# A graph network's message pass: one picked slot in twelve instead of fifteen, and an end that fetches its rows plainly and early

## The reference, cut to what matters

```python
def _L1_gnn_ref(node_feats, edge_index, edge_sh, edge_radial, W1, b1, ...):
    src, dst = (edge_index[0], edge_index[1])
    msg_input = jnp.concatenate([node_feats[src], edge_sh, edge_radial], axis=-1)   # 64 + 9 + 8
    h = jax.nn.silu(msg_input @ W1 + b1)          # 128
    h = jax.nn.silu(h @ W2 + b2)                  # 128
    messages = h @ W3 + b3                        # 64
    aggregated = jax.ops.segment_sum(messages, dst, num_segments=node_feats.shape[0])
    update_input = jnp.concatenate([node_feats, aggregated], axis=-1)
    gate = jax.nn.sigmoid(update_input @ G + gb)
    u = jax.nn.silu(_layernorm(update_input @ U1 + ub1, ln1_g, ln1_b))
    update = _layernorm(u @ U2 + ub2, ln2_g, ln2_b)
    return node_feats + gate * update
```

## Time and profile before

| | |
|---|---|
| median of 3 runs | 3172.85 us (3168.97 to 3183.3) |
| the profiled execution, its own time | 3195.68 us |
| its span, first to last instruction | 3194.0 us |
| mean granted TensorE clock | 0.925 of full |
| busy | PE 86%, DVE 60%, ACT 51%, POOL 47% |
| counting stage | 130 to 655 us |
| message pass | 1207 to about 3061 us |
| fetches of the end | 3063.7 to 3155.5 us |

### The profile page before, as it was taken

How to read it: one execution, slowest core, us unless ns; L and a number is a source line. 1 busy time by engine, 2 the same in 40 slices (tenths; PEclk the granted TensorE clock), 3 DMA queues, 4 the chain that set the end, 5 groups by cost and what they waited for, 6 DMA issues and landing times.

```text
span 3194.0 us, 63519 instructions
## 1 busy us (share of the span) xinstructions
PE 2752.0 (86%) x20761; PEld 2179.8 (68%) x20761; DVE 1919.2 (60%) x2346; ACT 1613.8 (51%) x2994; POOL 1515.6 (47%) x1572
## 2 busy tenths in 40 slices
PE   4499999967999985889888989888989898898975
PEld 3377777757998982666666666666767666676654
DVE  5899999964444564455555555555555555555526
ACT  2488888832332223455545555545555554555534
POOL 4000000000000006777777777777777777777765
PEclk9999999968999996899999999999999999999976
DMA  3133333326998973445444445544445555444421
GB/s 109 61 141 161 141 161 141 161 121 260 365 361 320 359 287 79 107 121 132 120 119 119 122 117 125 129 121 121 121 117 125 119 128 124 120 121 116 126 48 30
DMA packets 216659, 477.09 MB, mean 149 GB/s; under 512 B 53932, under 2 KB 114910, under 8 KB 197601
## 3 DMA queue, kind: packets, MB, share of 16 engines
q1 hardware_dynamic: 159976, 422.33, 38.5%
q0 software_dynamic: 55632, 52.47, 10.3%
q10 hardware_dynamic: 1001, 1.66, 0.1%
HBM read 339.87 MB, written 136.41 MB: 149 GB/s over the span
## 4 chain that ended last, share of the span: by engine, by line
PE 47%; POOL 25%; issue 11%; DVE 11%; DMA 4%; ACT 1%; DVEq 0%; POOLq 0%; ACTq 0%
POOL arena L663 22%; PE ps L791 14%; PE ps L961 8%; PE ps L810 6%; PE ps L973 5%; PE ps L980 5%; PE ps L988 5%; DMA arena<-m_tab,m_idx 3%; DVE arena L1868 2%; POOL ybuf L678 2%; PE ps L950 2%; DVE stageT L1844 2%; PE ps L706 1%; PE ps L694 1%; POOL arena L604 0%
## 5 line engine op out<-in xcount | busy, mean ns | idle before, releaser
L663 POOL DMA_INDIRECT arena<-m_tab,m_idx x1463 | 1391.4, 951 | 1586.0 <-issue 1574.8
L2118 DVE TENSOR_TENSOR_SCAN arena<-arena,ps 128x512 f32<-128x512 f32 x391 | 500.2, 1279 | 856.6 <-ACT ps L1335 723.4
L988 PEld LDWEIGHTS ps<-weights,arena 128*128 128x128 f32 x3128 | 438.2, 203 | 210.3 <-issue 196.4
L1330 ACT ACTIVATE arena<-ps,weights 128x512 f32<-128x512 f32 x391 | 268.7, 687 | 490.7 <-PE ps L973 483.1
L791 PE MATMUL ps<-arena 128*128 128x195 bf16 (+1 forms) x4802 | 481.5, 248 | 32.2 <-DVE arena L1810 31.6
L791 PEld LDWEIGHTS ps<-arena 128*128 128x128 f16 x4802 | 416.8, 98 | 62.8 <-DVE arena L1810 31.8
L961 PE MATMUL ps<-ends,arena 128*128 128x192 bf16 x4900 | 458.9, 252 | 0.0
L973 PE MATMUL ps<-arena,weights 81*128 81x512 f32 x782 | 443.5, 651 | 0.0
L980 PE MATMUL ps<-arena,weights 128*128 128x512 f32 x782 | 435.9, 640 | 0.0
L961 PEld LDWEIGHTS ps<-ends,arena 128*128 128x128 bf16 x4900 | 421.7, 100 | 7.0
L988 PE MATMUL ps<-weights,arena 128*128 128x64 f32 x3128 | 415.4, 279 | 1.7 <-ACT arena L1342 1.7
(11 more groups left out here) (269 smaller groups left out, 2294.1 us busy)
## 6 DMA issues: line engine op xcount, KB each, us to landing
arena<-count_d SPq DMA_DIRECT2D x98, 1568.0 KB, 8.5
arena<-keep_d SPq DMA_DIRECT2D x391, 256.0 KB, 3.9
count_d<-arena SPq DMA_DIRECT2D x49, 1568.0 KB, 5.1
scan_rows<-arena SPq DMA_DIRECT2D x391, 128.0 KB
arena<-m_tab,m_idx POOLq DMA_INDIRECT x1463, 3.3
arena<-attr_in SPq DMA_DIRECT2D x391, 34.0 KB
arena<-src_row SPq DMA_DIRECT2D x25, 258.0 KB
hT_d<-stageT ACTq DMA_DIRECT2D x12, 132.0 KB
```

Of the source, the lines that this page charges most:

```text
L663: pool.indirect_dma_start(m_rows[:, k, t, :], None, m_tab, bass.IndirectOffsetOnAxis(ap=m_idx[:, k, t:t + 1].bitcast(U32), axis=0))\
L988: last = pe.matmul(m_back[k % BACK_RING][:, t * D:(t + 1) * D], m_scan[:, k % SCAN_RING, t * P:(t + 1) * P], W("W3"), start=True, stop=True)
L2118: dve.tensor_tensor_scan(m_scan[:, k % SCAN_RING, :], m_mask[:, k % MASK_RING, :], m_term[k % TERM_RING], before, ALU.mult, ALU.add).then_ ...
```

## The change

- `LOOP` goes from 15 to 12: 33 laps instead of 27, 31 of them in the inner loop instead of 25, each with one picked slot. The first lap has 12 gathered slots instead of 15, the last 7 instead of 1. Rings are resized to divide 12.
- The nine picks of a lap stand in PE's slots 5 to 9, two each in four of them; the 0/1 pieces are made in DVE's slots 0 to 3 (three, two, two, two).
- The last four `rows_back` write to three PSUM banks instead of one.
- SP writes zeros to the last 20 slots of `scan_rows` once the masks are stored: 10240 rows of 256 bytes, all read from one row on one SBUF partition.
- The fetches of the end don't add any more. Each group waits only until as many slots are stored as its last node needs (a number that DVE computes and POOL loads into a register), so that they follow the last gather at once. DVE adds the b3 term, now kept in `hbuf`, per group (`add_b3`). POOL's adds to the residual rows stay behind all fetches.

```diff
-LOOP = 15
+LOOP = 12
-MASK_RING = 5
-ATTR_RING, TERM_RING, SCAN_RING, OUT_RING = 5, 3, 5, 5
+MASK_RING = 6
+ATTR_RING, TERM_RING, SCAN_RING, OUT_RING = 4, 3, 4, 4
+CLEARED = 20
-IDX_STEP = 5
+IDX_STEP = 4
-PICK_RING, PICK_BLOCKS, PICK_LAG = 3, 6, 5
+PICKS_AT = {5: (0, 1), 6: (2, 3), 7: (4, 5), 8: (6, 7), 9: (8,)}
+MARKS_AT = {0: (0, 1, 2), 1: (3, 4), 2: (5, 6), 3: (7, 8)}
+JOIN_AT = 7
...
             sp.wait_ge(masks_stored, 6 * DMA)
+            sp.dma_start(scan_rows[(NSLOT - CLEARED) * BE:NSLOT * BE, :], zero_row[:, :].unsqueeze(1).to_broadcast([1, CLEARED * BE, D]))\
+              .then_inc(zero_stored, DMA)
...
-            for k in range(OUT_RING):
-                pool.wait_ge(e1.stored[k], DMA * ((NSLOT - k + OUT_RING - 1) // OUT_RING))
             for i, (a, n) in enumerate(END_GROUPS):
+                needed = slots_needed[P - 1:P, a + n - 1:a + n]
+                pool.wait_ge(e1.turn_done, LOOP * (LAPS - 1) + fetch_slots[i] + 1 + (LOOP if fetch_slots[i] < LAST else 0))
+                pool.wait_ge(e1.out_ready, pool.to_reg(pool.value_load(needed, min_val=OUT_RING + 1, max_val=NSLOT + OUT_RING)))
+                pool.sem_inc(alone, 1)
                 for j in range(a, a + n):
                     pool.indirect_dma_start(ybuf[:, j, :], None, scan_rows,
-                                            bass.IndirectOffsetOnAxis(ap=end_idx[:, j:j + 1].bitcast(U32), axis=0),
-                                            compute_op=ALU.add).then_inc(rows_fetched[i], DMA)
+                                            bass.IndirectOffsetOnAxis(ap=end_idx[:, j:j + 1].bitcast(U32), axis=0))\
+                        .then_inc(rows_fetched[i], DMA)
...
-                    if PICK_LAG <= k < PICK_LAG + len(PICKS):
-                        pick_rows(i, k - PICK_LAG)
+                    for n in PICKS_AT.get(k, ()):
+                        pick_rows(i, n)
...
+            def add_b3(i, a, n):
+
+                dve.wait_ge(rows_fetched[i], fetched[i] + n * DMA)
+                dve.tensor_tensor(ybuf[:, a:a + n, :], ybuf[:, a:a + n, :], hbuf[:, a:a + n, :], ALU.add).then_inc(agg_ready, 1)
```

More of the change, by code:

```diff
@@ L258, in build @@
         m_back = [ps[:, 2 + TERM_RING, k * TB * D:(k + 1) * TB * D] for k in range(BACK_RING)]
+        last_back = [ps[:, 2 + TERM_RING + k % 3, 0:TB * D] for k in range(LAG)]
         def W(name):
@@ L397, in late_block @@
             return first % RING, first // RING + k + 1, first + RING * k
-        update_ready, hT_stored, hT_loaded, let_in = (sem(n) for n in ("update_ready", "hT_stored", "hT_loaded", "let_in"))
+        update_ready, hT_stored, hT_loaded, agg_ready = (sem(n) for n in ("update_ready", "hT_stored", "hT_loaded", "agg_ready"))
         agg_turned, agg_copied, agg_multiplied = (sem(n) for n in ("agg_turned", "agg_copied", "agg_multiplied"))
-        rows_fetched = e1.gathered[1:1 + len(END_GROUPS)]
-        FETCHED = DMA * TB * (LAPS - 1)
+        fetch_slots = [*range(LAST, PICKED), *range(1, 1 + len(END_GROUPS) - (PICKED - LAST))]
+        rows_fetched = [e1.gathered[k] for k in fetch_slots]
+        fetched = [DMA * TB * (LAPS if k < LAST else LAPS - 1) for k in fetch_slots]
         u_ready, u_squared, u_staged, u_turned, u_done, gate_done, v_done, v_added, v_squared = (sem(n) for n in (
             "u_ready", "u_squared", "u_staged", "u_turned", "u_done", "gate_done", "v_done", "v_added", "v_squared"))
+        let_in = sem("let_in")
         zero_ready, zero_stored = sem("zero_ready"), sem("zero_stored")
@@ L563, in move_slot @@
                     load_mask(s - LAG + MASK_RING, (k - LAG) % MASK_RING)
+            sp.wait_ge(zero_stored, 2 * DMA)
             for k in range(LOOP):
@@ L575, in _ @@
                 store_rows_of(s, s % OUT_RING)
+            for k in range(OUT_RING):
+                sp.wait_ge(e1.stored[k], DMA * ((NSLOT - k + OUT_RING - 1) // OUT_RING))
+            sp.sem_inc(e1.out_ready, OUT_RING)
             for i, (a, n) in enumerate(END_GROUPS):
@@ L980, in hidden_out, with rows_back @@
                 pe.matmul(m_term[k % TERM_RING], W("W2"), m_hid[:, k % HID_RING, :], start=True, stop=True).then_inc(e1.w2_done, 1)
-            def rows_back(s, k, late):
+            def rows_back(s, k, late, to=m_back[0], ring=BACK_RING):
                 pe.wait_ge(e1.scan_done, s + 1)
                 if late:
-                    pe.wait_ge(e1.out_ready, s - BACK_RING + 1)
+                    pe.wait_ge(e1.out_ready, s - ring + 1)
                 for t in range(TB):
-                    last = pe.matmul(m_back[k % BACK_RING][:, t * D:(t + 1) * D], m_scan[:, k % SCAN_RING, t * P:(t + 1) * P], W("W3"),
+                    last = pe.matmul(to[:, t * D:(t + 1) * D], m_scan[:, k % SCAN_RING, t * P:(t + 1) * P], W("W3"),
                                      start=True, stop=True)
@@ L1018, in _ @@
                 hidden_out(s, s % LOOP, True)
-            for s in range(NSLOT - LAG, NSLOT):
-                rows_back(s, s % LOOP, True)
+            for n, s in enumerate(range(NSLOT - LAG, NSLOT)):
+                rows_back(s, s % LOOP, True, last_back[n], n + 1 if n < 3 else 3)
             flat = ones[:, :].bitcast(BF16)
@@ L1034, in turn_agg @@
                     keep_busy(3, 8)
-                pe.wait_ge(rows_fetched[i], FETCHED + n * DMA)
+                pe.wait_ge(agg_ready, i + 1)
                 for t in range(n):
@@ L1335, in second_silu, with rows_out @@
                 act.activation(m_term[k % TERM_RING], m_term[k % TERM_RING], ACT.Silu, bias=W("b2")).then_inc(e1.silu2_done, 1)
-            def rows_out(s, k, lap):
+            def rows_out(s, k, lap, of=m_back[0]):
                 act.wait_ge(e1.back_done, s + 1)
@@ L1368, in _ @@
                 second_silu(s, s % LOOP)
-            for s in range(NSLOT - LAG, NSLOT):
-                rows_out(s, s % LOOP, s // LOOP)
+            for n, s in enumerate(range(NSLOT - LAG, NSLOT)):
+                rows_out(s, s % LOOP, s // LOOP, last_back[n])
             def square_u(i, a, n):
@@ L2140, in _ @@
                     scan_slot(LOOP * i + k, k, i)
-                    if k < len(PICKS):
-                        mark_pick(i, k)
+                    for n in MARKS_AT.get(k, ()):
+                        mark_pick(i, n)
             for k in range(LAST):
```

19 lines of the change are left out of this document (14 added, 5 removed).

## The result

The changed kernel takes 3149.24 us (median of 20 runs, 3133.78 to 3170.45), the kernel before 3184.72 us on the same chips (20 runs, 3168.64 to 3195.43). The ratio is 0.9902, 95% interval 0.9882 to 0.9922: 1.0% faster. The time forecast was 3149 us, and that agreement is luck. The forecast said 24 us less, and measured were 35.5 us less; the three runs from which it started (median 3172.85) lay 12 us under the median of the 20, which hides just this. The profiled execution says the same as the medians: span 3158.3 us against 3194.0, 35.7 less.

A forecast was written before the change was run, and what follows sets the result against it. POOL's gathers were taken to bound the message pass, and the fetches the node update at the end. Loop -30, end -26 and zeros +32 gave -24 from 3172.85 to 3149 us; forecast's own range 3135 to 3168, overall 3110 to 3204.

The forecast's parts named there:

- The loop, -30: Message pass: 1439 gathers instead of 1463, 24 fewer at 1.25 us, -30.0 us if PE keeps up.
- 4.6 us of slack: Message pass: PE needs 50.4 us of POOL's 55.0 us lap, so slack falls from 10.8 to 4.6 us.
- the pieces just in time: Message pass: DVE makes each 0/1 piece in 1.80 us with 2 us available, so picks hold with little to spare.
- The risk that was given 0.04: Message pass, rival 3: PE becomes the loop's bound and gathers wait for its turnings, +81 us, 3230 us; chance 0.04.
- The end, -26: From last gather's end to span's end: 124 us instead of 150.0, with fetches no longer kept waiting; bounds -34 and -10.
- first bias add T + 27: End: DVE's first bias add comes 27 us after T, the end of the last gather, where it was T + 39.
- eight steps 72: End, node update: nine groups have eight steps between them, taken at 9.0 us each, 72 us.
- The write of zeros, +32: Before the counting stage's block stores: a 94 us write delays block 0 and stops ACT at block 2, +32 us.
- The bound of 298 us: Write of zeros: upper duration for one source partition, by doubling from a 64-partition load of 11.4 us.
- The formula: Write of zeros: start 87 + duration 94 + landing 5.1 - 154.1, when ACT begins block 2, gives +32 us.
- Rival 1: Write of zeros is hidden, lasting 62 us or less: -56, 3117 us; chance 0.25.
- Rival 4: End: the update keeps today's pace of 11.0 us a step, losing 16 us of the gain, 3165 us; chance 0.09.

The follow-up runs named there:

- the version with 128 partitions: Changed kernel with its zeros read from a zero row in each of 128 partitions instead of one: median 3107.2 us, ratio to before 0.9767.
- the four kernels with a stop: Changed kernel, and it with the zero row 128 B further on, with 2 KB pieces, or with ACT issuing the write: medians 3149.2, 3145.0, 3145.1, 3158.9 us.
- the two kernels with 27 GB/s in SP's queue: Changed kernel with the zero row 128 B further on, or with zeros in 2 KB pieces, both from one partition: ratios to before 0.9871 and 0.9880.

## Why the prediction was right, and where it was not

**The loop, -30: right.** Measured -32.1 us; four more traces have 1802.2 to 1804.5 us. The premise of 4.6 us of slack in a lap on PE held (4.1 waited), and so did the pieces just in time. The risk that was given 0.04, gathers that wait for PE's turnings, is real on a chip that holds PE back, and was not thought of as a matter of the chip.

**The end, -26: right in kind, too small; -47.0.** The terms, forecast against measured: first bias add T + 27 against T + 20.7; eight steps 72 against 60.1; the add rows 2 more, not seen apart; last bias add to the end 23.2 against 22.1. Two terms were mis-sized. The first is the way to the first bias add: the last turning back ended at T + 12.5 instead of T + 14.4, and with PE at work the granted clock stood at 1.00 between 3060 and 3110, where in before it was 0.67 from 3054 to 3064, so that the filler went in 4.5 us instead of 6.0 and the first turning reached its bias add in 4.0 us instead of 6.7. The prediction let the clock pass for a thing that "may" rise.

The larger one, 12 us, is the duration of a group's step: 9.0 us forecast, 7.5 on the mean. It was read from two steps of before as if their data had been ready. Four windows, each from one bias add to the next: the 8.9 us step of before, the fifth and the seventh step of after, and the seventh with 128 partitions:

```profile
3106.03:3114.94 8.91, 4.72 (x36) 4.22 (x34) 4.99 (x9) 5.87 (x9) 7.39 (x6) 1.00 0.21 18
```

```profile
3103.78:3111.74 7.96, 5.35 (x39) 4.82 (x37) 7.51 (x16) 6.24 (x9) 6.13 (x7) 0.98 0.15 28
3119.95:3128.30 8.35, 3.71 (x25) 3.12 (x26) 8.11 (x15) 6.03 (x9) 2.88 (x3) 1.00 0.21 76
```

```profile
3061.46:3069.81 8.35, 6.33 (x25) 5.59 (x26) 8.11 (x16) 6.03 (x9) 2.88 (x3) 0.59 0.21 76
```

In the step of before DVE was busy 5.0 of 8.9 us and PE 4.7, and the steps beside it took 12.8 and 14.1: these three went at the pace of the fetches, 11.0 us a group, or slower, and were no measure of the update's own work. (The other step that was read, 8.3 us, is the last one, of a small group; it took 7.9 in after.) In after DVE is busy 7.3 to 8.1 us in each step from the fourth to the seventh, which take 7.6 to 8.4, so DVE's work sets them. The clock does not: the seventh step takes 8.35 us at 1.00 and at 0.59 alike. The first two take 6.5 us, with DVE busy 4.0 and 4.5; the normalising of earlier groups comes in only later. The register loads that the prediction put at 0.8 us a group leave no idle time that shows (0.30 us between fetches, 49 times); 49 fetches end 63 us behind T instead of 68. What ends last now is DVE, with the fetches close behind: DVE waited 0.2 us for one at 3111.2.

**The write of zeros, +32: right in kind, too small; +43.5.** The term that was mis-sized is its duration: 94 us, scaled from a table store of 512 such rows, against 113.6. That 94 lies so near is in part luck: nothing in the table store has to do with a single source partition, which is what sets the time. (The bound of 298 us is no bound either: it doubles the 64-partition time four times, and from 64 partitions to one are six doublings.) The formula with the measured figures gives 85.3 + 113.6 + 5.1 - 154.1 = 49.9, and the last block store is 50.6 us later. Of that 7.1 us came back before the first gather. This was not foreseen: the 90 us behind the last block store had the clock at 0.56 before and 0.72 after. The gain comes only with a stop (from the last block store to first gather 553.2 us in before and 554.6 with 128 partitions, 545.2 to 546.3 in the four kernels with a stop). That a stop leaves something of the clock for later is the reading; the rows show no more than that they go together.

The two errors, 11.5 us too little cost and 21 too little gain, partly cancel, and with 2 us of the loop the sum was 11.7 us too cautious. The low start of the three runs then took off the same 12 us. Rival 1 (3117 us) was wrong for this kernel, and it is what the version with 128 partitions turned out to be, at 3107. Rival 4 is refuted by the steps of 6.5 to 8.4 us.

## What to carry to other kernels

A fill from a single partition ran at 27 GB/s at best, in pieces of 256 B and of 2 KB; give the source all 128 partitions, and look at what stands behind it in any queue. Where the duration of a step is copied from a trace, look first whether any engine was busy for all of it: if none was, something else set the pace, here the fetches, and the engine with the most work in it gives the better estimate. Where PE's products are in the chain, look at the granted clock of that stretch too. A change that trades POOL's time for PE's is worth what the slack on PE is worth on the slowest chip that it will run on.

## What the runs showed of the hardware that was not expected

- PE's first products ran at two rates in different executions with the granted clock given as 1.00 in both. The window 50 to 60 us, after and then the version with 128 partitions:

```profile
50.00:60.00 10.00, 10.00 (x45) 8.63 (x45) 2.41 (x4) 1.82 (x2) 7.68 (x8) 1.00 0.29 84
```

```profile
50.00:60.00 10.00, 10.00 (x86) 9.21 (x84) 3.56 (x6) 3.00 (x4) 7.67 (x8) 1.00 0.30 85
```

  A product took 421 ns on the mean in the one and 275 in the other, and the second reached the write of zeros 12.6 us sooner. That this makes a good part of the spread of the runs is likely but not shown, since the other executions left no trace.
- Beside the slow write the counting stage began later. With the write under way its first work on ACT began at 118.6 us instead of 114.1, at 121.9 and 122.2 in the two kernels with 27 GB/s in SP's queue, and at 118.1 with the write in ACT's, after an idle time that the profile gives to "issue". With the write over it began at 100.2, with everything else 12.6 us sooner. That the loading of code is what is delayed is a guess.
- Chips differ by far more than kernels: 3183, 4375 and 4438 us for the same kernel. In the traces of its variants nearly all of that lies in the message pass, 2976 to 3099 us from first to last gather against some 1804. On the slow chips PE, ACT and DVE stand for long stretches while POOL starts plain indirect transfers 1.25 us apart; on the other chip they do not.
- A store in a free queue needed 54.3 us instead of 5.1 beside a slow write in another.
